# Orders of work behind a selective scan, with two routed blocks begun inside the scan's last step

## The reference

```python
mod = (_silu(L0_c) @ L0_wmod).reshape(B, 6, 1, -1)         # sa, ca, ga, sb, cb, gb
h = _layernorm(x) * (1 + ca) + sa
x = x + ga * attn(h)                                        # Mamba, forward and backward, D_STATE 16
h = _layernorm(x) * (1 + cb) + sb
x = x + gb * ffn(h)
# in attn, per direction:
h = h * exp(dt_t * A) + (dt_t * u_t) * B_t ;  y = sum_n h * C_t        # the scan over time
y = (y + xc * D) * silu(z) @ W_out.T
# ffn:
scores = softmax(xt @ gate_w.T); top_vals, idx = top_k(scores, 2)
y = sum_e mask_e * ((silu(xs @ w1[e].T + b1[e]) @ w2[e].T + b2[e]) * (xs @ w3[e].T + b3[e]))
z = silu(xt @ sw1.T) * (xt @ sw2.T) @ sw3.T                 # shared expert
```

## Time and profile before

| | |
|---|---|
| median of 3 runs | 2078.44 us (2076.93 to 2078.99) |
| profiled execution, its own time | 2083.13 us |
| its span, first to last instruction | 2081.4 us |
| mean granted TensorE clock | 0.918 of 2.4 GHz |
| end of the last scan | 1668.7 us into the span |
| first expert matmul | 1863.9 us |
| busy: PE, DVE, ACT, POOL | 88%, 93%, 77%, 86% of the span |

### The profile page before, as it was taken

How to read it: one execution, slowest core, us unless ns; L and a number is a source line. 1 busy time by engine, 2 the same in 40 slices (tenths; PEclk the granted TensorE clock), 3 DMA queues, 4 the chain that set the end, 5 groups by cost and what they waited for, 6 DMA issues and landing times.

```text
span 2081.4 us, 25376 instructions
## 1 busy us (share of the span) xinstructions
PE 1822.1 (88%) x6768; PEld 830.6 (40%) x6768; DVE 1927.3 (93%) x1829; ACT 1596.7 (77%) x3355; POOL 1790.9 (86%) x609
## 2 busy tenths in 40 slices
PE   7888898989898978888898889898977689999997
PEld 3322333424242323233333323242422256569996
DVE  7898999999999999999999999999999987757775
ACT  5886879898989888877779898989885734446664
POOL 5689999999999999999999999999999923535555
PEclk9889898989898989899898989898978899999999
DMA  7746454444535353626354544445353365335654
GB/s 265 235 124 148 105 139 114 124 113 121 126 107 132 104 132 94 162 68 158 91 140 104 137 113 127 118 119 127 94 117 103 104 218 211 124 103 90 95 93 73
DMA packets 140654, 263.93 MB, mean 127 GB/s; under 512 B 21841, under 2 KB 44369, under 8 KB 139489
## 3 DMA queue, kind: packets, MB, share of 16 engines
q1 hardware_dynamic: 125920, 240.58, 43.2%
q0 software_dynamic: 13296, 17.80, 5.1%
q10 hardware_dynamic: 1296, 3.93, 0.5%
HBM read 193.10 MB, written 70.19 MB: 126 GB/s over the span
## 4 chain that ended last, share of the span: by engine, by line
PE 27%; ACT 22%; DVE 19%; issue 16%; POOL 14%; DMA 1%; DVEq 0%; ACTq 0%; POOLq 0%; SPq 0%; PEldq 0%
DVE hst L1864 13%; POOL hst L1040 9%; ACT psum L1382 8%; DVE dbu L1843 5%; PE psum L2395 4%; POOL dbu L1028 4%; PE psum L2616 3%; PE psum L2771 3%; PE psum L2780 3%; PE psum L2791 3%; ACT dbu L1414 3%; PE psum L2630 2%; PE psum L2315 1%; ACT sp_tmp L1351 1%; ACT dt L1346 1%
## 5 line engine op out<-in xcount | busy, mean ns | idle before, releaser
L1040 POOL TENSOR_TENSOR hst<-hst,c_rep 128x2048 f32<-128x2048 f32 x254 | 1145.5, 4535 | 3.4 <-ACT state L1368 3.0
L1382 ACT ACTIVATE psum<-dt_rep,neg_a 128x512 f32<-128x512 f32 (+1 forms) x1024 | 659.8, 675 | 126.2 <-DVE hst L1864 121.9
L1864 DVE TENSOR_TENSOR_SCAN hst<-psum,state,dbu 128x1024 f32<-128x1024 f32 x264 | 604.5, 2331 | 0.4 <-DVE score L1940 0.4
L1864 DVE TENSOR_TENSOR_SCAN hst<-psum,dbu 128x1024 f32<-128x1024 f32 x248 | 555.0, 2273 | 10.7 <-ACT psum L1382 7.8
L1843 DVE TENSOR_TENSOR dbu<-psum,b_rep 128x2048 f32<-128x2048 f32 x177 | 401.0, 2266 | 9.3 <-PE psum L2380 9.3
L1028 POOL TENSOR_TENSOR dbu<-dtu_rep,b_rep 128x2048 f32<-128x2048 f32 x79 | 359.2, 4547 | 14.5 <-DVE hst L1864 8.8
L2395 PE MATMUL psum<-hst,same 128*32 128x512 f32 x2048 | 270.8, 676 | 48.7 <-POOL hst L1040 48.7
L2380 PE MATMUL psum<-dt,same 32*128 32x512 f32 x354 | 215.2, 690 | 104.1 <-DVE dbu L1843 94.7
L2327 PE MATMUL psum<-xp,taps 128*128 128x512 f32 x512 | 237.6, 607 | 5.8 <-ACT sp_tmp L1348 5.7
L1172 POOL DMA_INDIRECT out_x<-h,target_u x71 | 111.3, 1568 | 107.7 <-issue 54.9
L1414 ACT ACTIVATE dbu<-first_decay,dbu,state 128x1 f32<-128x1 f32 x504 | 160.0, 376 | 21.6 <-DVE dbu L1843 20.0
(11 more groups left out here) (223 smaller groups left out, 2608.9 us busy)
## 6 DMA issues: line engine op xcount, KB each, us to landing
dt_rep<-dt_scratch SPq DMA_DIRECT2D x256, 256.0 KB, 4.8
dtu_rep<-dtu_scratch SPq DMA_DIRECT2D x316, 64.0 KB, 1.9
taps<-taps_scratch SPq DMA_DIRECT2D x64, 256.0 KB, 4.3
b_rep<-bc_scratch SPq DMA_DIRECT2D x64, 256.0 KB, 5.0
c_rep<-bc_scratch SPq DMA_DIRECT2D x64, 256.0 KB, 7.8
dt_scratch<-dt SPq DMA_DIRECT2D x48, 256.0 KB, 6.2
h<-slot_scratch SPq DMA_DIRECT2D x71, 129.5 KB, 2.4
sp_tmp<-t_scratch SPq DMA_DIRECT2D x16, 512.0 KB, 6.9
```

The lines of the kernel that those rows point to most:

```text
L1040: nc.gpsimd.tensor_tensor(h, h, c_rep[q % 2][:], ALU.mult).then_inc(prod_done, 1)
L1382: nc.scalar.activation(psum[:, PS_A + i, kept], dt_rep[:, G % 2, j, kept], ACT.Exp, scale=neg_a[:, q % 2, u, i:i + 1]).then_inc(exp_done, 1)
L1864: nc.vector.tensor_tensor_scan(both(hst[:, U % RING, groups, :]), both(psum[:, PS_A + 2 * pair:PS_A + 2 * pair + 2, :]), both(dbu[:, U % D ...
```

## The change

Place 1 becomes early too (`EARLY = 2`): in step 15 it is added, normalised, turned and routed, and the shared expert's gate chunks `g1` are made; its ups (`u1_part`) come at the scan's end, into the decay banks. Place 0's pieces come three to four units earlier. POOL's constants move from between the units to behind the scan. Its residual for place 1 takes the room. One `spread_input` (the multiply's input of unit 247) moves ahead of a `sum_chunk`. All orders behind the scan on PE, DVE and ACT, and SP's loads, are rewritten.

```diff
-G0_AT = [(11, 3), (12, 3), (13, 3), (14, 0)]
-U0_AT = [(14, 3), (15, 0), (15, 2)]
+G0_AT = [(9, 1), (10, 0), (10, 1), (11, 0)]
+U0_AT = [(11, 3), (12, 1), (12, 2), (12, 3)]
+G1_AT = [(14, 2), (15, 0)]
```

PE, in step 15:

```diff
+                if t == 8:
+                    router_early(0)
+                    hidden_early("g", 0, sw1, 0)
                 if t == 9:
-                    for kd in range(KD):
-                        turn0(kd)
+                    hidden_early("g", 0, sw1, 1)
+                    hidden_early("g", 0, sw1, 2)
...
+                    turn_early(1, 0)
+                    turn_early(1, 1)
                 if t == 14:
-                    hidden0("u0", sw2, 2)
-                    hidden0("u0", sw2, 3)
+                    router_early(1)
+                    hidden_early("g", 1, sw1, 0)
+                    hidden_early("g", 1, sw1, 1)
+                if t == 15:
+                    hidden_early("g", 1, sw1, 2)
+                    hidden_early("g", 1, sw1, 3)
+                    turn_logits1()
...
+                if T == SPARED - 2:
+                    spread_input(T + 2)
                 if t % GN == 1 and T > GN:
                     sum_chunk(T // GN - 1)
```

POOL, in step 15:

```diff
+                if q == STEPS - 1 and t == 7:
+                    add_mixed(1)
...
-                    if t == 6:
+                    if t == 5:
                         pool.wait_ge(f_const, 1)
                         norm_power(0)
-                        scale_mean()
-                    constants(t)
+                        scale_mean(0)
+                        weigh_mixed(1)
+                    if t == 8:
+                        norm_power(1)
+                        scale_mean(1)
```

ACT, in step 15:

```diff
+            def copy_turned_early(p, kd):
+                if p == 0:
+                    act.wait_ge(prod_done, UNITS * (STEPS - 1))
+                    act.wait_ge(f_gate_loaded, 48)
+                else:
+                    act.wait_ge(chunk_summed, NC * STEPS - 1)
...
+                if (t, n) == (10, 3):
+                    normalise_tokens(1)
...
+                if (t, n) == (13, 3):
+                    copy_turned_early(1, 0)
+                    copy_turned_early(1, 1)
```

DVE, in step 15:

```diff
-                if t == 12:
+                if t == 8:
+                    norm_statistics(1)
+                if t == 11:
                     shift_logits(0)
```

PE, behind the scan:

```diff
-            out_0(0)
-            out_0(1)
-            turn(1)
-            shared_hidden(0, 1)
+            u1_part(0)
+            u1_part(1)
+            u1_part(2)
+            u1_part(3)
+            out_early(0, 0)
+            out_early(0, 1)
+            out_early(1, 0)
+            turn(2)
+            out_early(1, 1)
+            pe.wait_ge(s_o_mul, 2)
             sum_chunk(ALL_UNITS // GN - 1)
+            shared_hidden(0, 2)
+            shared_part(1, 2, False)
+            project_out(STEPS - 1, 0)
             pe.wait_ge(f_const, F_CONST)
             count_places(0)
-            project_out(STEPS - 1, 0)
-            router(1)
+            shared_part(2, 2, False)
             project_out(STEPS - 1, 1)
```

PE, its last part:

```diff
             out_end(6)
-            turn_logits(7)
+            count_places(7)
             out_second(6)
-            count_places(7)
-            for c in range(NC):
-                shared_hidden(c, 7)
+            shared_part(1, 7, False)
+            shared_part(0, 7, True)
+            shared_part(1, 7, True)
+            shared_part(2, 7, False)
+            shared_part(3, 7, False)
+            shared_part(2, 7, True)
+            shared_part(3, 7, True)
```

ACT, its last part:

```diff
-            scale_tokens(6, 1)
-            exp_scores(7)
             silu_shared(0, 7)
+            silu_shared(1, 7)
             scale_tokens(7, 0)
-            silu_shared(1, 7)
             silu_shared(2, 7)
+            silu_shared(3, 7)
             scale_tokens(7, 1)
-            silu_shared(3, 7)
```

More of the change, by code:

```diff
@@ L2714, in _ @@
[L2714 to L2716 removed]
+            out_end(2)
+            out_second(2)
+            turn_logits(2)
+            shared_part(2, 3, False)
+            shared_part(3, 3, False)
+            turn(4)
+            shared_part(0, 3, True)
+            shared_part(1, 3, True)
+            count_places(2)
+            shared_part(2, 3, True)
+            shared_part(3, 3, True)
+            router(3)
+            shared_part(0, 4, False)
```

814 lines of the change are left out of this document (449 added, 365 removed).

## The result

| | before | after |
|---|---|---|
| median | 2078.72 us (4 runs) | 2092.59 us (4 runs, 2092.09 to 2093.16) |
| ratio | | 1.0062, 95% interval 1.0051 to 1.0074 |
| profiled execution, own time (span) | 2083.13 us (2081.4) | 2092.55 us (2090.8) |
| last step of the scan, T = 240 to 255 | 109.94 us | 121.25 us |
| scan's end to the first expert matmul | 195.25 us | 194.83 us |

A forecast was written before the change was run, and what follows sets the result against it. DVE was taken to bound the scan's last step, with POOL full, and PE the stretch to the experts. Terms from -8.4 to +12.5 summed to +2.0 us, median 2080.4; forecast range 2077 to 2084, with rivals 2066 to 2087.

The forecast's parts named there:

- The scan's end: Last step of the scan: DVE's terms were to make the scan end 4.2 us later, bounds 2.5 to 6.
- unit 250's second half: In the scan's last step, DVE was to wait 2.7 us for decays behind ACT's copies of place 0's gate chunks.
- The second half of unit 246: In the scan's last step: its decays stand behind a copy of PE's z products, charged 0.5 us.
- a second place points to the same hour: Copies of place 1 at unit 253, awaiting chunk 62's sum, would replace a smaller first wait, up to some 3.5 us.
- PE's work behind the scan: Scan's end to experts: gate chunks, turning, router and logits gone, -8.4 us; first 32 records at a better clock, -2.7.
- The first new wait: Behind the scan, PE waits for DVE's last weighings ahead of the sum of chunk 63: +3.5 us.
- The large new wait: PE at turn(4): place 5's load lands late behind the weights and holds DVE ahead of norm_end(4): +12.5 us.
- The wait for the ranking: Behind turn(4), PE's count_places(2) waits for DVE's two shared sums, a shift and a ranking: +2.4 us.
- rival 2: PE's clock falls in the wait at turn(4) and stays low behind it: 2.7 us added, 2083.1 us; chance 0.20.
- the old waits: PE's earlier waits between its first matmul behind the scan and the experts go: -4.8 us.
- The tail: Ahead of the experts: ACT's last scale_tokens, behind the fourth silu, widens PE's gap from 0.9 to 2.0 us: +1.1.
- Rival 1: Place 5's load is in by about 1730, so 12.5 and 2.4 us fall away: 2065.5 us; chance 0.22.

The follow-up runs named there:

- e3: Changed kernel with place 0's last two ups chunks ahead of the input of unit 254 on PE: 2085.51 us, 1.0031 to before.
- e4: Changed kernel with place 0's second gate chunk ahead of chunk 61's sum on PE and the third's copy behind unit 250's decays on ACT: 2090.98 us.
- e7: Changed kernel with place 0's last two ups chunks ahead of unit 254's input, and its gate chunks and copies reordered around units 250 and 251: 2093.02 us, 1.0011.
- e14: Kernel before, unchanged, run and profiled again: 2081.83 us, 1.0007 to before.
- e1: Changed kernel with SP sending place 5's loads right behind place 4's, ahead of the last store of sums and the experts' weights: 2081.48 us, 1.0005 to before.
- e2: Changed kernel with add_mixed(5) moved behind place_tokens(2) in DVE's list, transfers untouched: 2080.32 us, 1.0008 to before.
- e6: Changed kernel with the last place's scalings on ACT and tables on DVE moved earlier: 2102.07 us, 1.0053 to before.
- e17: Changed kernel with the last place's ACT scalings and DVE tables earlier, third run of this edit alone: 2101.62 us, 1.0062 to before.
- e9: Changed kernel with the last place's ACT scalings and DVE tables earlier, second run of this edit alone: 2095.85 us, 1.0053 to before.

## Why the prediction was wrong

The forecast was 2080.4 us, +2.0; measured is 2092.59, +13.9 on the medians and +10.9 by the two stages.

- **The scan's end, +4.2 forecast, +11.3 measured: the step that failed.** By the rows: waits for decays 11.5, place 1's statistics 1.9 in series, less the 2.2 of before. Of the terms, the statistics (1.9) and unit 250's second half (2.7, measured 1.98) and its follower (0.8, measured 1.11) were near. The second half of unit 246 was put at 0.5 and is 1.49. The waits that the forecast names, with unit 248, come to 4.9 us where it had 4.5; unit 249 adds 0.6, and the other 6.1 are those at units 253 and 254, which it put at nothing. Its reason was the sentence "a second place points to the same hour ... so if the first wait is smaller, the second takes its place". I computed that place from POOL alone and let it stand as a floor that adds nothing. I didn't walk PE's list between POOL's weighing and the sum. There stand two up chunks behind an input that waits for DVE's next multiplication, and the sum is behind them. e3 measures this at 6.4 us. (The floor itself was also added up wrongly: its terms give 1662.5, not 1663.4.) e4 and e7 show that the reasoning on floors itself was right, with other members: repair one place alone and the next one takes most of it.
- **PE's work behind the scan, -8.4 and -2.7 for the clock: right.** The first 32 output records took 7.07 instead of 9.59. PE is busy for 11.9 us less; in that are 2.6 us of ups that it makes ahead of the scan's end, less 2.3 that its low clock behind the large wait costs.
- **The first new wait, +3.5: measured 2.1** (0.3 at `turn(2)`, 1.8 at the last sum).
- **The large new wait, +12.5: right in place and cause, measured 15.0.** The last `store_sum` came 43.2 us behind the scan (43.1 forecast); the weights went out 4.8 behind it, not 3.0, and the transfer 0.7 more. PE reached `turn(4)` 65.6 behind the scan, 65.5 forecast.
- **The wait for the ranking, +2.4: right in size, in another form.** From the start of `turn(4)` to `count_places(2)` it took 7.2 us, 6.7 forecast. PE stood still for only 0.4 of it, since rival 2's condition came true: its granted clock behind the wait was 0.66, with the turn at 1.97 instead of 1.04 and two chunks at 5.01 instead of 3.60, 2.3 us more. But the ranking ended 6.5 us behind the turn's start. At the high clock PE would have been done with the chunks near 1764.4 (my estimate: 1760.95 and 3.60 without the overlap) and would have waited till 1765.1 for it. So the low clock cost at most 0.7 us there, and the forecast's reason for charging nothing holds. The Trainium skill (TensorE: Matmul & The Clock Gate, "HAM oscillation — how this bites in real kernels") names just this, half clock after a gap, and the rows agree with it.
- **The five blocks without a wait, and the old waits (-4.8): right.**
- **The tail, +1.1: measured 2.0** in the gap, and some 2 us more inside the experts' first tiles, at 0.52 granted clock, which the forecast has nowhere.
- **The baseline.** I took the profiled execution of before, 2083.1, to lie 4.7 us above its median for every stage alike, and carried that over as a difference. e14 gives the same two stages within 0.1 us in a span 3.6 us shorter, so the change is read by stages. Of the 3.0 us that the first comparison has beyond them, the experts' first tiles are a part (0.5 to 2.7 us in that stage); the rest isn't explained. Four runs of before lie between 2076.93 and 2080.78, and 10.9 us is within the interval of the ratio.
- **The range.** Rival 2 with the scan at its bound of 6 gives 2084.9 us, not 2087.

Sum: 7.1 us from the scan, 1.8 from the parts behind it up to the experts, 3.0 beyond these two stages, and 0.3 by which the median of before has moved since: the 12.2 missed. Rival 1 gave the load's worth as 14.9; e1 and e2 measure 11.6 and 10.7, since 3 to 5 us come back at the next place.

## What to carry to other kernels

When a copy is put between the instructions that feed the bound engine, walk the producer's whole list back to its last wait, not just the product itself: here the wait was for an input of the bound engine's own next unit, two rows ahead, so that the bound engine waited for itself. Two stalls that seem to be alternatives need both chains written out before one is taken as free. And a late transfer can be mended where it is waited for as well as where it is issued: moving one pair of additions in DVE's list gave 10.7 us, moving the load 11.6.

## What the runs showed of the hardware

PE's results reached ACT and DVE late in three of the five batches, in stretches with scatters. Here is ACT's copy of the last router's logits and that router on PE, in the changed kernel's first profile:

```profile
1835.60 0.64 PE L2699 MATMUL psum<-h2T,gate 128*32 128x128 f32 x16
1836.31 0.28 ACT L1710 ACTIVATE turned_logits<-psum 128x128 f32<-128x128 f32 x1 [4.00 <-PE psum L2699]
```

and in e6, whose lists are the same up to this place:

```profile
1837.23 0.64 PE L2699 MATMUL psum<-h2T,gate 128*32 128x128 f32 x16
1839.18 0.96 POOL L1153 DMA_INDIRECT slot_scratch<-send,slot_u  x1 [0.30 <-issue]
1841.89 0.28 ACT L1710 ACTIVATE turned_logits<-psum 128x128 f32<-128x128 f32 x1 [7.68 <-remote]
```

The copy follows the router at once in the first. In e6 it starts 4.0 us behind the router's end and 1.8 behind the last of the scatters, and the trace names no engine of this core as releaser. Every run of batches 2, 3 and 5 has this at two copies of logits or more, by 1.6 to 4.0 us; none of batches 1 and 4 has it (0.1 us or less), edited or not. So it goes with the batch and not with the edits, and it accounts for e6 and e17 taking 207 us behind the scan where the changed kernel takes 195: in e6 PE waits for such results 11.4 us and is busy 2.9 us longer, less the 2.0 saved ahead of the experts. In these batches the kernel before, too, took 2085 to 2090 us instead of 2080; it has no profile there. My expectations speak of noisy and quiet chips; that isn't shown, since batches 1 and 3 carry the same chip number and only one of them has it. What delays the hand-over is open: in e9 DVE's late `add_shared` began before the last scatter had ended. Kernels that differ by 0.3% can only be compared within a batch.
